# Attention rows, keys and skip weights as f16 high and low parts, with their splits and the early block sums on GpSimd

## The chip, the cores and the metric

The kernel runs on one core of a Trainium2 chip (trn2). The metric is the device time of one launch in microseconds (us), as the median of several executions. Engines are named as in the profile: PE is TensorE (matmuls), PEld its weight loads, DVE VectorE, ACT ScalarE, POOL GpSimd, SP SyncE, whose queue issues most DMAs.

## The reference

The input `x` is 16 batches of 128 channels by 1024 columns (f32), with a context of 128 by 256 for each. The first half is a cross-attention, the second a gated feed-forward with 4-bit weights:

```python
# x: (16, 128, 1024), ctx: (16, 128, 256), all weights of the attention 128 x 128
xn = layernorm(x)                                    # over the 1024 columns
q, k, v = Wq @ xn, Wk @ ctx, Wv @ ctx
att = softmax(q.T @ k / sqrt(128))                   # 1024 x 256 for each batch
x = x + Wskip @ xn + v @ att.T
h = silu(layernorm(x) @ Wg.T) * (layernorm(x) @ Wu.T)   # 2752 wide, dequantized weights
x = x + h @ Wd.T
```

## The kernel before, in words

The kernel has two phases. The attention phase goes through the 16 batches in steps 0 to 16 (`STEPS`), pipelined over the engines with an order written out by hand for each engine; semaphores join them. The feed-forward phase, some 1150 us of the span, multiplies in f16 high and low parts with a seven-product scheme for 2 by 2 blocks; the change does not touch it.

In step i of the attention phase, in program order on each engine:

- PE: `energies(i, 0)` (four products of 128 rows of the normalized batch, as weights, against 256 columns of keys), `block_transposed` of a "between" block, `values(i-1, 0)` (one skip product of 512 columns, L548, then two products with the transposed probabilities, L553), `energies(i, 1)`, `probs_transposed(i-1, 1)`, `keys_values(i+1)`, `block_transposed` of an "after" block, `values(i-1, 1)`, `probs_transposed(i, 0)`. The keys are folded with the query weights, so that energies need only the row `xn` and the keys `kk`.
- DVE: `maxima(i, 0)` (L1294), the sums and low parts of the "between" block (L1319, L1300), `normalize(1, i-2)` (L1277), `inverse_total(i, 0)` (L1336), `add_attention(i-1, 0)` (L1332), `normalize(0, i+1)` (L1277), `maxima(i, 1)`, `row_stats(0, i+2)` (L1263, L1267), in some steps a piece of the first feed-forward weights (`meanwhile`: two operations or one of 1024 elements in the steps 4 to 8 and 11 to 14), `inverse_total(i, 1)`, the sums and low parts of the "after" block, `add_attention(i-1, 1)`, `row_stats(1, i-1)`.
- ACT: `block_hi` of the between block, a cast of one block sum (`sum_hi`, L852), `exponentials(i, 0)` (L833), `normalize_probs(i, 0)` (L859), `probs_out(i-1, 1)` (L825), `exponentials(i, 1)`, `block_hi`, `keys_out(i+1)` (L815), another `sum_hi`, `values_out(i+1)` (L819), `probs_out(i, 0)`, `normalize_probs(i, 1)`. After steps 9 and 13 it casts feed-forward weights as well (L902, L904, L909).
- POOL: from step 5 on the low part of a block sum (`sum_lo`, L407), `inverse_deviation(0, i+2)` (L398, L401: the reciprocal deviation of the row two batches ahead, which waits for `row_stats(0, i+2)`), a second `sum_lo`, `inverse_deviation(1, i-1)`.
- SP: loads of rows and context, stores of finished rows.

Layout: `xn` has three buffers of 1024 f32 columns, the keys two of 256. `T1` to `T4` are the block sums of the feed-forward phase; each pair of batches k makes four of them, written by DVE as f32 into the last columns of their own f16 buffer (`mixed`), then cast (high part) and subtracted (low part).

## Time and profile before

| what | value |
|---|---|
| three runs | 1405.16, 1405.92, 1406.82 us, median 1405.92 us |
| span of the profiled execution, first to last instruction | 1403.7 us, 2.2 us below that median |
| PE busy | 1384.9 us (99%), 6414 matmul records |
| DVE busy | 1116.8 us (80%) |
| ACT busy | 689.1 us (49%) |
| POOL busy | 309.5 us (22%) |
| granted TensorE clock | 1.000 of 2.4 GHz |
| attention phase (steps 0 to 16) | about the first 215 us |

The profile lists an f32 matmul as two records of equal length, an f16 matmul as one. Instructions overlap at their ends, so that the distance from one start to the next is what an operation costs in a full stream. The profiled execution has no time of its own beside its span; the three runs are other executions, and the 2.2 us between the span and their median is what lies around the span.

### The profile page before, as it was taken

Reading aid. Unit: us, or ns where it says so; the run is one execution under the profiler, and the core shown is the slowest. Engines: PE = TensorE matmul, PEld = TensorE weight load, DVE = VectorE, ACT = ScalarE, POOL = GpSimd, SP = SyncE. Lnnn points to the kernel's source line nnn. Section 1 sums busy time; section 2 is a strip of 40 time slices with the busy share of each in tenths; the row PEclk is TensorE's granted clock in tenths of the full one; section 3 lists DMA queues with packets and bytes.
Section 4 is the critical chain, followed back from the end, with each engine's and each line's share of the span. In section 5 each row is a group of like instructions: output and inputs, shape, how many; then the busy total and the mean of one; then the engine's idle time right before and its main releaser. Section 6 shows DMA issues by size and latency. Waiting matters only on the chain.

```text
span 1403.7 us, 19579 instructions
## 1 busy us (share of the span) xinstructions
PE 1384.9 (99%) x6414; PEld 677.0 (48%) x6414; DVE 1116.8 (80%) x1598; ACT 689.1 (49%) x1279; POOL 309.5 (22%) x365
## 2 busy tenths in 40 slices
PE   8999998999999999999999999999999999999999
PEld 6676764444444444444444444444444444444443
DVE  6888978887877778878788788788788788787476
ACT  6899984344344444444444444444444444434430
POOL 1132332132122122122222212222212212212200
PEclk9999999999999999999999999999999999999999
DMA  5222222286477576576666756846846746848796
GB/s 191 102 102 87 83 91 61 53 158 120 98 143 126 103 137 115 101 143 112 119 130 113 131 111 115 148 94 123 133 105 122 125 104 121 141 91 150 121 303 256
DMA packets 58983, 174.83 MB, mean 125 GB/s; under 512 B 8001, under 2 KB 11073, under 8 KB 54593
## 3 DMA queue, kind: packets, MB, share of 16 engines
q0 software_dynamic: 34560, 83.90, 39.1%
q1 hardware_dynamic: 24096, 90.20, 20.7%
q8 instruction: 19, 0.31, 0.1%
q10 hardware_dynamic: 288, 0.26, 0.1%
q14 instruction: 20, 0.16, 0.0%
HBM read 73.67 MB, written 100.66 MB: 124 GB/s over the span
## 4 chain that ended last, share of the span: by engine, by line
PE 91%; DVE 4%; ACT 3%; issue 2%; POOL 0%; DMA 0%; SPq 0%; DVEq 0%; POOLq 0%; ACTq 0%
PE ps L590 52%; PE ps L629 9%; PE ps L628 9%; PE ps L630 9%; PE ps L553 3%; PE ps L523 2%; PE ps L793 2%; PE ps L511 2%; PE ps L548 1%; PE ps L542 1%; ACT temps L859 1%; ACT temps L833 1%; PE ps L752 1%; DVE stats L1263 0%; DVE neg_max L1294 0%
## 5 line engine op out<-in xcount | busy, mean ns | idle before, releaser
L590 PE MATMUL ps<-xt,w_gu 128*128 128x512 f16 x3528 | 796.1, 379 | 5.7 <-DVE temps L1510 1.7
L590 PEld LDWEIGHTS ps<-xt,w_gu 128*128 128x128 f16 x3528 | 344.6, 98 | 422.8 <-ACT temps L939 2.6
L972 ACT ACTIVATE stage<-ps,pow 128x512 f32<-128x512 f32 x300 | 204.2, 686 | 320.0 <-PE ps L630 318.3
L1540 DVE SCALAR_TENSOR_TENSOR stage<-ps,pow,stage 128x512 f32<-128x512 f32 x220 | 160.0, 746 | 101.3 <-ACT stage L972 63.0
L628 PE MATMUL ps<-park 128*128 128x512 f16 x560 | 212.3, 379 | 0.0
L629 PE MATMUL ps<-park 128*128 128x512 f16 x560 | 212.3, 379 | 0.0
L630 PE MATMUL ps<-park 128*128 128x512 f16 x560 | 212.3, 379 | 0.0
L437 POOL DMA_DIRECT2D out<-stage x80 | 70.5, 881 | 424.1 <-DVE stage L1540 424.1
L451 POOL DMA_DIRECT2D out<-stage x80 | 69.0, 863 | 297.4 <-ACT stage L972 297.4
L969 ACT CAST park<-temps 128x512 f16<-128x512 f32 x140 | 83.1, 614 | 64.8 <-DVE temps L1524 38.1
L1537 DVE TENSOR_TENSOR park<-temps,park 128x512 bf16<-128x512 f32 x140 | 98.3, 708 | 17.0 <-ACT park L969 14.0
L630 PEld LDWEIGHTS ps<-park 128*128 128x128 bf16 x560 | 54.8, 98 | 66.1
L628 PEld LDWEIGHTS ps<-park 128*128 128x128 f16 x560 | 54.7, 98 | 66.1
L629 PEld LDWEIGHTS ps<-park 128*128 128x128 f16 x560 | 54.7, 98 | 66.1
L444 POOL DMA_DIRECT2D out<-stage x60 | 66.2, 1103 | 4.8 <-DVE stage L1540 4.5
L523 PE MATMUL ps<-w_gu,park 128*128 128x256 f32 x256 | 60.5, 380 | 2.2 <-ACT w_gu L815 1.5
L833 ACT ACTIVATE temps<-ps,neg_max 128x256 f32<-128x256 f32 x128 | 58.9, 475 | 6.3 <-DVE neg_max L1287 3.8
L553 PE MATMUL ps<-temps,w_gu 128*128 128x512 f32 x128 | 60.3, 594 | 1.0 <-ACT temps L825 1.0
L467 POOL TENSOR_TENSOR temps<-temps 128x512 f32<-128x512 f32 x20 | 30.7, 1535 | 124.2 <-DVE temps L1530 124.2
L1396 DVE TENSOR_TENSOR w_gu<-raw,w_gu 128x1024 f16<-128x1024 f32 (+1 forms) x43 | 52.0, 1209 | 7.7 <-ACT w_gu L909 6.1
L859 ACT ACTIVATE temps<-temps,inv_total 128x256 f32<-128x256 f32 x128 | 54.7, 502 | 4.9 <-DVE inv_total L1336 4.9
L523 PEld LDWEIGHTS ps<-w_gu,park 128*128 128x128 f32 x256 | 47.4, 190 | 14.7 <-issue 7.2
(137 smaller groups left out, 1622.2 us busy)
## 6 DMA issues: line engine op xcount, KB each, us to landing
out<-stage POOLq DMA_DIRECT2D x80, 512.0 KB, 5.3
out<-stage POOLq DMA_DIRECT2D x140, 256.0 KB, 5.4
grid<-grids SPq DMA_DIRECT2D x136, 256.0 KB, 6.0
raw<-packed SPq DMA_DIRECT2D x34, 512.0 KB, 4.3
out<-stage SPq DMA_DIRECT2D x16, 512.0 KB, 2.7
stage<-x SPq DMA_DIRECT2D x12, 512.0 KB, 3.5
xt<-out SPq DMA_DIRECT2D x12, 512.0 KB, 11.7
out<-xt SPq DMA_DIRECT2D x12, 512.0 KB, 2.6
```

Of the source, the lines that this page charges most:

```text
L437: pool.dma_start(out[t, :, 0:NOUT], stage[:, d % 2, 0:NOUT], accum_op=ALU.add).then_inc(s_add11[d % 2], 16)
L523: mm = pe.matmul(ps_e[f][:, t, :], xn[b % XNS][:, cols], kk[:, par, :], start=True, stop=True)
L553: mm = pe.matmul(ps_o, v_t[:, par, h, :], prob_t[:, f, h, :], start=False, stop=(h == 1))
L590: mm = pe.matmul(bank, w_gu[e][:, wp, w, P * j:P * j + P], xt[:, xb, xp, j, cols], start=(fresh and n == 0), stop=(n == 3 * J - 1), skip_g ...
L628: pe.matmul(bank, h_hi[:, h, rows], w_d[:, 0, w, :], start=fresh, stop=False, skip_group_check=not fresh)
L629: pe.matmul(bank, h_hi[:, h, rows], w_d[:, 1, w, :], start=False, stop=False, skip_group_check=not fresh)
L630: return pe.matmul(bank, h_lo[:, h, rows], w_d[:, 0, w, :], start=False, stop=True, skip_group_check=not fresh)
L833: ex = act.activation(prob[:, NTH * f + t, :], ps_e[f][:, t, :], ACT.Exp, bias=neg_max[:, f, t:t + 1], accum_out=total[:, f, t:t + 1])
L969: act.copy(h_hi[:, block, :], src).then_inc(s_h_hi, 1)
L972: return act.activation(dst, ps[:, bank, :], ACT.Copy, scale=pow2[:, 10:11])
L1537: dve.tensor_tensor(h_lo[:, block, :], src, h_hi[:, block, :], ALU.subtract).then_inc(s_h_lo, 1)
L1540: return dve.scalar_tensor_tensor(out=part, in0=ps[:, bank, :], scalar=pow2[:, 10:11], in1=part, op0=ALU.mult, op1=ALU.add)
```

## The change

From batch 2 on (`SPLIT`) the attention keeps its operands as f16 pairs, a high part and what is left:

- The row: DVE's `normalize(0, b)` writes the f16 high part in place of the f32 row. POOL computes the f32 row again into a scratch area (`xn_exact`) and subtracts the high part from it (`split_row`).
- The keys: ACT writes f32 keys to a scratch area, POOL casts them (`kk_hi`) and subtracts (`kk_lo`), in `split_keys`.
- The skip weights are split once on POOL (`split_skip`).
- PE multiplies energies and skip as three f16 products each (high by high, low by high, high by low) in place of one f32 product. `energies(i+1, 0)` begins with a wait for `s_kk_hi`, then waits for `s_xn_lo` and `s_kk_lo` ahead of its second and third group.
- The high-part casts of the block sums of the first six pairs of batches go from ACT (`sum_hi`) to POOL (`sum_parts`). The other eight stay on ACT.
- Two waits for buffers: DVE's `bn_aggr` of row b waits until POOL has computed `xn_exact` of row b-2, and ACT's `keys_out(b)` until `kk_lo` of batch b-1 is done.

The core of the diff:

```diff
+            def split_row(b):
+                n = b - SPLIT + 1
+                hi, lo = xn_parts[b % XNS][:, 0, :], xn_parts[b % XNS][:, 1, :]
+                pool.wait_ge(s_rstd[0], b + 1)
+                wait(pool, s_xn_lo, n - 1)
+                pool.tensor_scalar(xn_exact, row(b).rearrange("p (c r) -> p c r", c=8), mv[:, 0, b % 2, 0:1],
+                                   rstd[:, 0, b % 2:b % 2 + 1], ALU.subtract, ALU.mult).then_inc(s_xn_exact, 1)
+                pool.wait_ge(s_xn, b + 1)
+                pool.wait_ge(s_xn_exact, n)
+                pool.tensor_tensor(lo.rearrange("p (c r) -> p c r", c=8), xn_exact,
+                                   hi.rearrange("p (c r) -> p c r", c=8), ALU.subtract).then_inc(s_xn_lo, 1)
+
+            def split_keys(b):
+                n = b - SPLIT + 1
+                hi, lo = kk_parts[:, b % 2, 0, :], kk_parts[:, b % 2, 1, :]
+                pool.wait_ge(s_kk_sb, b + 1)
+                pool.tensor_copy(hi, kk_exact).then_inc(s_kk_hi, 1)
+                pool.wait_ge(s_kk_hi, n)
+                pool.tensor_tensor(lo, kk_exact, hi, ALU.subtract).then_inc(s_kk_lo, 1)
...
+            def sum_parts(k, u):
+                pool.wait_ge(s_mixed, nth_sum(k, u) + 1)
+                pool.tensor_copy(xt_of(k, u, 0).rearrange("p j (h r) -> p j h r", h=2),
+                                 mixed(k, u).rearrange("p (j h) r -> p j h r", h=2)).then_inc(s_sum_cast, 1)
+                sum_lo(k, u)
...
             for i in range(1, STEPS):
                 k = (i - 5) // 2
                 if k >= 0:
-                    sum_lo(k, T2 if i % 2 == 0 else T3)
+                    sum_parts(k, T2 if i % 2 == 0 else T3)
+                if i + 1 < B:
+                    split_row(i + 1)
                 if i + 2 < B:
                     inverse_deviation(0, i + 2)
                 if i % 2 and k >= 0:
-                    sum_lo(k, T1)
+                    sum_parts(k, T1)
                 elif k >= 0:
-                    sum_lo(k, T4)
+                    sum_parts(k, T4)
+                if i + 1 < B:
+                    split_keys(i + 1)
                 inverse_deviation(1, i - 1)
...
+                n = b - SPLIT + 1
                 if f == 0:
-                    pe.wait_ge(s_kk_sb, b + 1)
                     pe.wait_ge(s_xn, b + 1)
+                    pe.wait_ge(s_kk_hi, n)
+                pe.wait_ge(s_exp, 2 * b + f - 1)
+                for xp, kp in ((0, 0), (1, 0), (0, 1)):
+                    if f == 0 and xp:
+                        pe.wait_ge(s_xn_lo, n)
+                    if f == 0 and kp:
+                        pe.wait_ge(s_kk_lo, n)
+                    for t in range(NTH):
+                        cols = slice(P * (NTH * f + t), P * (NTH * f + t) + P)
+                        mm = pe.matmul(ps_e[f][:, t, :], xn_parts[b % XNS][:, xp, cols], kk_parts[:, par, kp, :],
+                                       start=(xp + kp == 0 and t % 2 == 0), stop=(kp == 1), skip_group_check=True)
...
-                k = (i - 3) // 2
...
-                if k >= 1:
-                    sum_hi(k - 1, T1 if i % 2 else T4)
...
-                if i % 2 == 0 and k >= 0:
-                    sum_hi(k, T3)
-                elif k >= 1:
-                    sum_hi(k - 1, T2)
+                if i == B:
+                    sum_hi(LAST - 1, T3)
...
+                if which == 0:
+                    wait(dve, s_xn_exact, b - SPLIT - 1)
```

## Rows read from the trace of the kernel before

**Rows 1.** Busy time of each engine in the nine periods from step 5 to step 14
```profile
core 0: us, PE busy (x) PEld busy (x) DVE busy (x) ACT busy (x) POOL busy (x), PEclk, DMA share, GB/s
64.45:177.26 112.81, 111.75 (x524) 78.61 (x523) 100.81 (x206) 107.88 (x309) 39.51 (x54) 1.00 0.25 89
```

**Rows 2.** Pieces of the chain that ended last (start us, us, what)
```profile
130.85 0.52 ACT xt L852
...
179.65 1.88 ACT w_gu L909 x2
```

**Rows 3.** Timeline of PE: first energies of steps 2, 5, 9, 10, 11, 14, 15
```profile
28.10 1.89 PE L523 MATMUL ps<-w_gu,park 128*128 128x256 f32 x8
...
64.45 1.89 PE L523 MATMUL ps<-w_gu,park 128*128 128x256 f32 x8
...
114.11 1.89 PE L523 MATMUL ps<-w_gu,park 128*128 128x256 f32 x8
...
126.53 1.89 PE L523 MATMUL ps<-w_gu,park 128*128 128x256 f32 x8
...
140.02 1.89 PE L523 MATMUL ps<-w_gu,park 128*128 128x256 f32 x8
...
177.26 1.89 PE L523 MATMUL ps<-w_gu,park 128*128 128x256 f32 x8
...
191.17 1.89 PE L523 MATMUL ps<-w_gu,park 128*128 128x256 f32 x8
```

**Rows 4.** Timeline of PE: an f32 skip product, and twelve f16 products
```profile
116.31 1.02 PE L548 MATMUL ps<-park,w_gu 128*128 128x512 f32 x2
...
202.47 2.75 PE L590 MATMUL ps<-xt,w_gu 128*128 128x512 f16 x12
```

**Rows 5.** Timeline of step 9: DVE, POOL and ACT
```profile
116.24 1.17 DVE L1294 TENSOR_REDUCE neg_max<-ps 128x4 f32<-128x1024 f32 x1
...
117.25 1.16 POOL L407 TENSOR_TENSOR xt<-xt 128x512 f16<-128x512 f32 x1
...
118.52 0.81 DVE L1277 TENSOR_SCALAR park<-stage,mv,rstd 128x1024 f32<-128x1024 f32 x1
...
119.47 0.18 DVE L1336 RECIPROCAL inv_total<-total 128x4 f32<-128x4 f32 x1
...
120.14 0.81 DVE L1277 TENSOR_SCALAR park<-stage,mv,rstd 128x1024 f32<-128x1024 f32 x1
...
120.86 1.22 DVE L1294 TENSOR_REDUCE neg_max<-ps 128x4 f32<-128x1024 f32 x1
...
123.68 0.19 POOL L398 TENSOR_TENSOR var_eps<-mv,eps 128x1 f32<-128x1 f32 x1 [5.26 <-DVE mv L1267]
...
124.46 1.16 POOL L407 TENSOR_TENSOR xt<-xt 128x512 f16<-128x512 f32 x1
...
124.52 0.42 ACT L815 ACTIVATE w_gu<-ps 128x256 f32<-128x256 f32 x1
```

**Rows 6.** Timeline: DVE and POOL operations that overlap
```profile
86.21 1.18 DVE L1386 TENSOR_TENSOR raw<-raw,grid 128x1024 f32<-128x1024 int32 x1
...
86.44 1.00 POOL L398 TENSOR_TENSOR var_eps<-mv,eps 128x1 f32<-128x1 f32 x1 [6.13 <-DVE mv L1267]
...
149.79 0.46 POOL L398 TENSOR_TENSOR var_eps<-mv,eps 128x1 f32<-128x1 f32 x1 [5.22 <-DVE mv L1267]
...
150.32 1.42 POOL L401 TENSOR_TENSOR rstd<-var_eps,neg_half 128x1 f32<-128x1 f32 x1
...
206.91 1.15 POOL L407 TENSOR_TENSOR xt<-xt 128x512 f16<-128x512 f32 x1 [0.47 <-ACT xt L852]
...
207.55 1.06 DVE L1277 TENSOR_SCALAR park<-w_gu,mv,rstd 128x1024 f32<-128x1024 f32 x1
```

**Rows 7.** Timeline of POOL at the start: operations with one input or none
```profile
0.76 0.20 POOL L386 MEMSET ident<- 128x128 f32 x1
...
1.50 0.30 POOL L389 TENSOR_SCALAR_AFFINE_SELECT ident<-ident 128x128 f32<-128x128 f32 x1 [0.50 <-POOL eps L387]
```

More of the change, by code:

```diff
@@ L76, in nth_sum @@
     return 4 * k + SUMS.index(u)
+EARLY_SUMS = 4 * (LAST - 1)
 def uses_of_step(i):
@@ L97 @@
 XNS = 3
+SPLIT = 2
 LATER = 2
@@ L143, in build @@
         xn = [park[:, N * k:N * k + N] for k in range(3)]
+        xn_parts = [t.bitcast(F16).rearrange("p (a n) -> p a n", a=2) for t in xn]
         xn2 = park[:, 3072:7168].rearrange("p (s n) -> p s n", s=XNS2)
         x12 = more[:, :].rearrange("p (c r) -> p c r", c=8)
-        last_columns = xt[:, :, :, :, :].rearrange("p u a j t -> p u (a j) t").bitcast(F32)[:, :, :, (GT - P) // 2:]
+        xt_words = xt[:, :, :, :, :].rearrange("p u a j t -> p u (a j) t").bitcast(F32)
+        last_columns = xt_words[:, :, :, (GT - P) // 2:]
+        xn_exact = xt_words[:, X11, :, (GT - 2 * P) // 2:]
         def mixed(k, u):
@@ L223, in build @@
         s_xn = sem("s_xn")
+        s_xn_exact = sem("s_xn_exact")
+        s_xn_lo = sem("s_xn_lo")
+        s_kk_hi = sem("s_kk_hi")
+        s_kk_lo = sem("s_kk_lo")
+        s_skip_hi = sem("s_skip_hi")
+        s_skip_lo = sem("s_skip_lo")
+        s_sum_cast = sem("s_sum_cast")
         s_xn2 = sem("s_xn2")
@@ L410, in sum_lo @@
                                    ).then_inc(s_sum_lo, 1)
+            def sum_parts(k, u):
[3 more added lines that the diff above has]
+                sum_lo(k, u)
             inverse_deviation(0, 0)
             inverse_deviation(0, 1)
+            split_skip()
             inverse_deviation(0, 2)
@@ L516, in energies @@
                 par = b % 2
+                if b < SPLIT:
+                    if f == 0:
+                        pe.wait_ge(s_kk_sb, b + 1)
+                        pe.wait_ge(s_xn, b + 1)
+                    wait(pe, s_exp, 2 * b + f - 1)
+                    for t in range(NTH):
+                        cols = slice(P * (NTH * f + t), P * (NTH * f + t) + P)
+                        mm = pe.matmul(ps_e[f][:, t, :], xn[b % XNS][:, cols], kk[:, par, :], start=True, stop=True)
+                        if b == 0 and f == 0 and t == 1:
+                            mm.then_inc(s_first_energy, 1)
+                    mm.then_inc(s_energy, 1)
+                    return
+                n = b - SPLIT + 1
                 if f == 0:
-                    pe.wait_ge(s_kk_sb, b + 1)
                     pe.wait_ge(s_xn, b + 1)
-                wait(pe, s_exp, 2 * b + f - 1)
-                for t in range(NTH):
-                    cols = slice(P * (NTH * f + t), P * (NTH * f + t) + P)
-                    mm = pe.matmul(ps_e[f][:, t, :], xn[b % XNS][:, cols], kk[:, par, :], start=True, stop=True)
-                    if b == 0 and f == 0 and t == 1:
-                        mm.then_inc(s_first_energy, 1)
+                    pe.wait_ge(s_kk_hi, n)
[5 more added lines that the diff above has]
+                        pe.wait_ge(s_kk_lo, n)
+                    for t in range(NTH):
+                        cols = slice(P * (NTH * f + t), P * (NTH * f + t) + P)
+                        mm = pe.matmul(ps_e[f][:, t, :], xn_parts[b % XNS][:, xp, cols], kk_parts[:, par, kp, :],
+                                       start=(xp + kp == 0 and t % 2 == 0), stop=(kp == 1), skip_group_check=True)
                 mm.then_inc(s_energy, 1)
@@ L547, in values @@
                 wait(pe, s_res, 2 * b + f)
-                pe.matmul(ps_o, w_att[:, 3, :], xn[b % XNS][:, H * f:H * f + H], start=True, stop=False)
+                cols = slice(H * f, H * f + H)
+                if b < SPLIT:
+                    pe.matmul(ps_o, w_att[:, 3, :], xn[b % XNS][:, cols], start=True, stop=False)
+                else:
+                    if b == SPLIT and f == 0:
+                        pe.wait_ge(s_skip_lo, 1)
+                    for n, (wp, xp) in enumerate(((0, 0), (1, 0), (0, 1))):
+                        pe.matmul(ps_o, w_skip[:, wp, :], xn_parts[b % XNS][:, xp, cols], start=(n == 0), stop=False)
                 if f == 0:
@@ L814, in keys_out @@
                 act.wait_ge(s_kv, b + 1)
-                act.mul(kk[:, b % 2, :], ring_bank(("keys", b))[:, 0:M], float(C) ** -0.5).then_inc(s_kk_sb, 1)
+                wait(act, s_kk_lo, b - SPLIT)
+                act.mul(kk[:, b % 2, :] if b < SPLIT else kk_exact, ring_bank(("keys", b))[:, 0:M], float(C) ** -0.5
+                        ).then_inc(s_kk_sb, 1)
             def values_out(b):
@@ L1275, in normalize @@
                     dve.wait_ge(s_xt_ps, NTH_UNIT[(b - XNS2) // 2, X22 if b % 2 else X21] + 1)
-                dst, done = ((xn[b % XNS], s_xn), (xn2[:, b % XNS2, :], s_xn2))[which]
+                first = xn[b % XNS] if b < SPLIT else xn_parts[b % XNS][:, 0, :]
+                dst, done = ((first, s_xn), (xn2[:, b % XNS2, :], s_xn2))[which]
                 dve.tensor_scalar(dst, row(b), mv[:, which, b % 2, 0:1], rstd[:, which, b % 2:b % 2 + 1],
```

14 lines of the change are left out of this document (13 added, 1 removed).

## The prediction

> **What bounds the kernel now.** I read the page first, which says that PE is busy 99% of the span, then the stretches, then the chain of waits, then the timeline of one step. The change touches only the attention, so what counts is the limit there. In the nine periods from `energies(5, 0)` to `energies(14, 0)` PE is busy 111.75 of 112.81 us, ACT 107.88, DVE 100.81, POOL 39.51 [rows 1]: PE is the limit, but ACT is only 4% below it and DVE 11%. A regular period is 126.53 - 114.11 = 12.42 us [rows 3]. Two periods are longer, 10 (140.02 - 126.53 = 13.49) and 14 (191.17 - 177.26 = 13.91) [rows 3]: there the chain of waits leaves PE and runs through ACT, which also casts feed-forward weights, 1.88 us of them in the second case [rows 2]. The clock is granted in full throughout [rows 1]. So relief for PE is worth something only down to where the next loop through ACT, DVE and POOL closes. I therefore cost PE's gain, and then that loop.
>
> **What PE saves.** The records of an f16 product of 512 columns follow each other every (2.75 - 0.38) / 11 = 0.215 us (0.38 being one record), while an f32 product of 512 columns is two records in 1.02 us, 0.43 each after the overlap [rows 4]. So f32 costs four times f16, and three f16 products cost three quarters. Skip: 0.86 to 0.65, saving 0.21, twice a batch. Energies: eight f32 records of half the columns, 0.215 each, are 1.73 us (1.89 with the end of the last [rows 3]); twelve f16 products of 256 columns at half of 0.215 are 1.30, saving 0.43, twice a batch. The trace has no f16 product of 256 columns; the bounds are this half and, were weight loads to hold it, a third more (1.7, no saving at all on the energies). I take the half, from the nearest row, in which each product loads weights of its own too. Sum: 1.29 us a batch, 14 batches, 18 us, if PE stays the limit (period 11.13).
>
> **What ACT saves.** Two casts of 0.52 us a step [rows 2], so from 107.88 / 9 = 11.99 to 10.95 us a period [rows 1]. ACT is then no limit, and the extra casts after steps 9 and 13 fit into its slack: the 13.49 and 13.91 lose their excess.
>
> **What POOL gets.** Today 39.51 / 9 = 4.4 us a period [rows 1]. A subtraction of 512 elements takes 1.16 [rows 5] and one element 0.19 [rows 5], so 1.9 ns an element: 2.13 for `xn_lo` (1024), 0.67 for `kk_lo` (256). Operations with one input are shown only at 128 elements, 0.30 and 0.20 us [rows 7]; with 0.19 at one element that is 0.9 ns an element: 0.62 for a cast of 512, 0.40 for `kk_hi`, 1.06 for `xn_exact`. These prices are the least certain. From above they are bounded by the two-input price (1.16, 0.67, 2.13), from below by a third of mine. I take mine, as nearest to the one-input rows, but 1.3 for `xn_exact`, which has two operations in it and two scalars from memory. Sum with turnarounds: 4.4 + 1.24 + 1.3 + 2.13 + 0.40 + 0.67 + 0.3 = 10.4 us a period, under 12.4.
>
> The Trainium skill, GPSIMD Engine Reference, section 3.1, gives the two-input operation about 2.6 cycles an element at 1.2 GHz, which the 1.16 us for 512 agrees with, and a good one-input loop 1.8 cycles. By 1.8 cycles the cast would be 0.77 and `xn_exact` 1.54, and the period below would be 0.4 us longer, some 3 us in all.
>
> **The loop that POOL closes.** Occupancy is not the point; order is. `energies(i+1, 0)` now waits for `kk_hi`, which stands in POOL's queue behind `inverse_deviation(0, i+2)` and a whole `sum_parts`. That deviation waits for `row_stats(0, i+2)`, which stands on DVE behind `maxima(i, 1)`, and so back to `energies(i, 0)`. Every link is in program order, so the length of the loop is a floor of the period from step 5 on:
> - energies start to first maxima: 11 x 0.108 + 0.28 + 0.04 = 1.50.
> - First to second maxima, with exponentials, reciprocal, addition and normalization between: 120.86 - 116.24 = 4.62 [rows 5].
> - Second maxima to the deviation: 123.68 - 120.86 = 2.82 [rows 5].
> - The deviation: 124.46 - 123.68 = 0.78 [rows 5].
> - The cast of the sum and its turnaround: 0.70. Its low part: 1.10. `kk_hi` and its semaphore: 0.45.
>
> Together 11.97 us. Before, only the wait for ACT's keys (ready 8.7 us after the first maxima [rows 5]) stood there, and PE came later than that.
>
> **Locks.** DVE's normalization and a running POOL operation exclude each other: at 207.55 it lasts 1.06 in place of 0.81 and ends 0.55 after POOL's operation ends (208.06) [rows 6]. It goes the other way too: L398 takes 1.00 in place of 0.19 under a DVE operation with two SBUF inputs, and at 149.79 the two deviation instructions take together 1.14 longer [rows 6]. I walk the loop with that. POOL is free 1.0 us after the first maxima (117.25 against 116.24) and then casts and subtracts until 2.9. The first normalization, due at 2.3 (118.52), waits and ends at 3.45, which delays the reciprocal (3.2 before) by about 0.3. `xn_exact` runs from 3.45 to 4.75. The second normalization, due at 4.2, ends at 5.3, and the second maxima start at 5.35 in place of 4.62. That is 0.73 us: period 12.70. With `xn_exact` at 1.06 it is 0.48. The Trainium skill, SBUF — State Buffer, section "Who interferes with whom", calls this pair of ports an exclusive lock for a whole instruction and names both kinds of DVE operation; the rows agree.
>
> In steps 5 to 8 and 11 to 13 DVE's weight work follows `row_stats` directly and delays the deviation by 0.81 to 1.14 [rows 6]. Before that cost nothing, POOL having 8 us idle in a period; now it stands in the loop. Seven steps at 0.85 are 5.9 us. `xn_lo` ends about 7.5 after the first maxima, ahead of the deviation, and DVE's new wait for `xn_exact` of two rows back is met a step early: both nothing; if POOL ran a step late they would add to the same delay.
>
> **The sum.** Steps 5 to 14: 9 x 12.70 + 5.9 = 120.2 against 112.81: +7.4. Period 14 has no deviation of a row 16, so `kk_hi` waits only for ACT's keys: 1.5 + 0.73 + 8.7 + 0.5 = 11.4, taken 11.8 against 13.91: -2.1 (from -2.5 to -0.6 if ACT's extra casts are not hidden). Steps 2 to 4 have no sums on POOL, loop 10.2, but DVE, busy 100.81 of 112.81 anyway [rows 1], holds them: 36.35 us for three periods [rows 3], -1.0 (from 0 to -3.9). After `energies(15, 0)` PE saves up to 1.3, of which DVE, on which the first feed-forward blocks wait, lets half come through: -0.5. Elsewhere nothing: the feed-forward is unchanged and only shifts. `split_skip` is 0.7 us on idle POOL in step 0. Together +3.8 on the span of 1403.7. The median of the runs lies 2.2 above the span, so 1405.92 + 3.8 = 1409.7 us.
>
> **The rivals.**
> 1. PE stays the limit (the other side). The loop would have to be shorter than 11.13. For it: DVE and ACT busy times of 11.2 and 10.95 would nearly allow it. Against it: the links without any new operation are already 1.50 + 4.62 + 2.82 + 0.78 = 9.72, and `sum_lo` makes it 10.8; cast and `kk_hi` would have to take 0.3 together, and no lock may bite. Time: 1405.9 - 18 = 1388.
> 2. The loop is there, but short: one-input operations at a third of my price, `xn_exact` out of DVE's way, period 11.6. 9 x 11.6 + 5.9 = 110.3, -2.5; with the other terms -6.1: 1400.
> 3. POOL's one-input operations cost as much as its two-input ones: cast +0.54, `kk_hi` +0.27, `xn_exact` until 6.1 and so 2.05 of locks. Period 14.83; POOL's own sum is then 12.6 plus locks, so that it is nearly full as well. 9 x 14.83 + 5.9 = 139.4, +26.6, with the rest +23: 1429.
> 4. Gain and loss cancel, DVE setting the pace with its busy 11.2 plus locks of about 1: period 12.3 to 12.4, 1405.
>
> **Chances.** Forecast 46% (its own range 1404 to 1415), rival 1 10%, rival 2 17%, rival 3 22%, rival 4 5%. A change within 0.2% (2.8 us) can't be told from none. Faster: rival 1 and six tenths of rival 2, 20%. Same: rival 4, the rest of rival 2 and 10% of the forecast, 22%. Slower: 58%. The range leaves out rival 1 and half of rival 3: 1399 to 1429.
>
> **What the profile of the changed kernel would show.** PE's energies of batch 2 on as 12 records in about 1.5 us: right on the first term. Idle time of PE ahead of the energies' first product, released by POOL `kk_hi`, about 1.5 us in each step from 5 on: the loop. None there and starts 11.1 apart: rival 1. Casts of 512 at 0.6 and `xn_exact` at 1.3: the prices; at 1.2 and 2.1: rival 3. DVE's L1277 longer than 0.81 in most steps: the lock. L398 near 1.0 in steps 5 to 8 with a later start of the energies: the last term. The forecast is wrong above all if a one-input operation of POOL costs something else, for each 0.1 us of the cast is about 1 us of the time.

## The result, and the profile after

The changed kernel takes 1431.67 us (median of four runs, 1429.37 to 1431.8), the kernel before 1405.75 in its runs beside it. The ratio is 1.0179, 95% interval 1.0167 to 1.019: 26 us slower. I had forecast 1409.7 with a range of 1399 to 1429, so the sign was right and the size was not. The span of the profiled execution is 1427.6 us, 23.9 above that of before. That execution was the shortest of the four (1429.37 us, mean granted clock 0.994; the others took 1431.54 to 1431.8 at 0.990 or 0.991), so the traces below account for 23.9 of the 26 us; for the other two there is no trace. For the same reason differences of medians and differences of profiled spans are told apart below.

The busy line of the profile's page and the busy times of the nine periods (from `energies(5, 0)` to `energies(14, 0)`), columns as in [rows 1]:

```profile
PE 1376.8 (96%) x6554; PEld 670.8 (47%) x6554; DVE 1128.8 (79%) x1598; ACT 678.3 (48%) x1255; POOL 429.2 (30%) x447
```

```profile
74.51:201.81 127.30, 104.76 (x614) 73.09 (x612) 112.02 (x209) 103.09 (x297) 115.67 (x109) 0.99 0.24 83
```

Over the span PE is still the busiest by far. In the nine periods it isn't: PE 104.76, DVE 112.02, ACT 103.09 and POOL 115.67 of 127.30 us. No engine is at 100%, and POOL, 39.51 in [rows 1], has become the fullest.

The timeline of PE, first energies of steps 2, 5, 6, 9, 10, 11, 14 and 15 (some groups are cut by the window's end), against [rows 3]. The profile names no releaser for the waits in brackets ("issue"); which one it was is read from the program order and from what GpSimd does just then:

```profile
38.37 2.71 PE L600 MATMUL ps<-w_gu,park 128*128 128x256 f16 x12 [10.37 <-issue]
...
74.51 1.47 PE L600 MATMUL ps<-w_gu,park 128*128 128x256 f16 x12
...
90.50 2.72 PE L600 MATMUL ps<-w_gu,park 128*128 128x256 f16 x12 [3.31 <-issue]
...
93.63 0.81 PE L631 MATMUL ps<-park,w_gu 128*128 128x512 f16 x3
...
119.10 1.47 PE L600 MATMUL ps<-w_gu,park 128*128 128x256 f16 x12 [2.97 <-issue]
...
132.62 1.14 PE L600 MATMUL ps<-w_gu,park 128*128 128x256 f16 x9 [1.93 <-issue]
...
146.09 1.14 PE L600 MATMUL ps<-w_gu,park 128*128 128x256 f16 x9 [1.99 <-issue]
...
201.81 1.60 PE L600 MATMUL ps<-w_gu,park 128*128 128x256 f16 x10 [3.08 <-issue]
...
215.67 1.47 PE L600 MATMUL ps<-w_gu,park 128*128 128x256 f16 x12 [0.90 <-issue]
```

Where the 23.9 us are, by differences of these starts and those of [rows 3], beside my terms:

| stretch | before | after | difference | my term |
|---|---|---|---|---|
| up to energies 5 | 64.45 | 74.51 | +10.06 | -1.0 |
| nine periods | 112.81 | 127.30 | +14.49 | +7.4 |
| step 14 | 13.91 | 13.86 | -0.05 | -2.1 |
| from energies 15 to the end | 1212.53 | 1211.93 | -0.60 | -0.5 |

So three things have to be explained: ten microseconds ahead of step 5, where I had put one less, seven more than forecast in the steady steps, and two more than forecast in step 14. For the second, the timeline of POOL over step 9:

```profile
132.12 0.40 POOL L445 CAST w_gu<-w_gu 128x256 f16<-128x256 f32 x1
132.60 0.67 POOL L447 TENSOR_TENSOR w_gu<-w_gu 128x256 f16<-128x256 f32 x1
...
134.64 0.61 POOL L462 CAST xt<-xt 128x512 f16<-128x512 f32 x1
135.33 1.16 POOL L455 TENSOR_TENSOR xt<-xt 128x512 f16<-128x512 f32 x1
136.47 4.30 POOL L434 TENSOR_SCALAR xt<-stage,mv,rstd 128x1024 f32<-128x1024 f32 x1
140.92 2.13 POOL L438 TENSOR_TENSOR park<-xt,park 128x1024 f16<-128x1024 f32 x1
...
143.80 0.61 POOL L462 CAST xt<-xt 128x512 f16<-128x512 f32 x1
144.49 1.16 POOL L455 TENSOR_TENSOR xt<-xt 128x512 f16<-128x512 f32 x1
145.59 0.40 POOL L445 CAST w_gu<-w_gu 128x256 f16<-128x256 f32 x1
```

From `kk_hi` to `kk_hi` it is 145.59 - 132.12 = 13.47 us, the period of PE (146.09 - 132.62 = 13.47), with one gap of 0.59 in it; PE's energies start 0.50 after the start of `kk_hi` both times. From 78 us on POOL has no longer gap than 1.1 us up to the end of the nine periods: its queue is full. Casts (0.61, 0.40) and subtractions (0.67, 1.16, 2.13) cost what I had said. L434, the recomputed row `xn_exact`, costs 3.8 to 4.3 us where I had put 1.3.

For the first, the timeline of POOL at the start:

```profile
23.21 0.40 POOL L471 PARTITION_ALL_REDUCE pow_tmp<-pow  x1 [5.67 <-issue]
31.01 3.80 POOL L434 TENSOR_SCALAR xt<-stage,mv,rstd 128x1024 f32<-128x1024 f32 x1 [7.40 <-issue]
34.95 2.12 POOL L438 TENSOR_TENSOR park<-xt,park 128x1024 f16<-128x1024 f32 x1
...
37.88 0.40 POOL L445 CAST w_gu<-w_gu 128x256 f16<-128x256 f32 x1
```

The split of row 2 and of its keys stands in POOL's queue behind a reduction over the partitions (it finds the scales of the feed-forward weights), which has a gap of 5.67 us ahead of it and one of 7.40 behind it. `energies(2, 0)` starts 0.1 us after the end of `kk_hi`, at 38.37 in place of 28.10. GpSimd's sequencer (POOLq) has two instructions without busy time at the start of each gap: at 17.51 and 17.54, of the reduction's line, and at 23.56 and 23.60, of the line that comes next. The second pair, in the view of that line up to 36 us:

```profile
L434 POOLq MODIFY_POOL_CONFIG  x2: 83/83/83, 23.6 to 23.6; - x2
```

### The profile page after: what moved, and what is told of

Read it like the earlier page. It is cut to its first block, busy times and chain, and to the rows that moved or that the text cites. A ratio compares the mean times of both kernels' runs of the same rounds, so it can differ in the third digit from the quotient of the medians.

```text
span 1427.6 us, 19970 instructions
## 1 busy us (share of the span) xinstructions
PE 1376.8 (96%) x6554; PEld 670.8 (47%) x6554; DVE 1128.8 (79%) x1598; ACT 678.3 (48%) x1255; POOL 429.2 (30%) x447
## 4 chain that ended last, share of the span: by engine, by line
PE 88%; DVE 5%; issue 4%; ACT 2%; DMA 0%; POOL 0%; SPq 0%; DVEq 0%; POOLq 0%; ACTq 0%
PE ps L673 51%; PE ps L711 8%; PE ps L713 8%; PE ps L712 8%; PE ps L636 2%; PE ps L876 2%; PE ps L600 2%; PE ps L835 1%; PE ps L570 1%; PE ps L618 1%; PE ps L631 1%; DVE neg_max L1377 1%; ACT temps L918 1%; ACT temps L944 1%; DVE park L1360 1%
## 5 line engine op out<-in xcount | busy, mean ns | idle before, releaser
L600 PE MATMUL ps<-w_gu,park 128*128 128x256 f16 x336 | 44.3, 285 | 32.4 <-issue 32.4
L1377 DVE TENSOR_REDUCE neg_max<-ps 128x4 f32<-128x1024 f32 x31 | 37.5, 1211 | 25.2 <-PE ps L600 25.1
```

Source lines behind the costliest of these rows:

```text
L600: mm = pe.matmul(ps_e[f][:, t, :], xn_parts[b % XNS][:, xp, cols], kk_parts[:, par, kp, :], start=(xp + kp == 0 and t % 2 == 0), stop=(kp ...
```

## The experiments

All are edits of the changed kernel except where noted. The table gives the median, the ratio to the kernel before with its 95% interval, the start of `energies(5, 0)`, the length of the nine periods, and the busy times in them. The last column but one is PE's granted clock there.

| run | us | ratio | energies 5 | nine periods | PE | DVE | ACT | POOL | clock | what |
|---|---|---|---|---|---|---|---|---|---|---|
| after | 1431.67 | 1.0179 | 74.51 | 127.30 | 104.8 | 112.0 | 103.1 | 115.7 | 0.99 | |
| e1_split3 | 1423.71 | 1.0128 (1.0111 to 1.0144) | 64.95 | 131.35 | 109.8 | 111.8 | 103.3 | 115.5 | 0.93 | split from batch 3 |
| e11_no_reduce | 1420.36 | 1.0109 (1.0094 to 1.0124) | 63.31 | 128.97 | 107.5 | 111.5 | 103.0 | 115.1 | 0.96 | no reduction |
| e2_exact_dve | 1424.15 | 1.0138 (1.0121 to 1.0155) | 71.45 | 125.46 | 105.9 | 110.0 | 100.1 | 78.3 | 0.97 | row on DVE |
| e3_no_pool | 1400.23 | 0.9964 (0.995 to 0.9979) | 63.10 | 109.54 | 102.4 | 102.3 | 98.4 | 49.3 | 1.00 | no splits |
| e4_casts_act | 1423.96 | 1.0136 (1.0119 to 1.0153) | 74.99 | 119.97 | 103.8 | 108.8 | 107.4 | 102.9 | 1.00 | sums' casts on ACT |
| e5_keys_first | 1425.97 | 1.0143 (1.0126 to 1.016) | 75.08 | 124.48 | 103.9 | 118.4 | 101.8 | 115.0 | 1.00 | keys ahead of sum |
| e6_dve_three | 1410.94 | 1.0036 (1.0023 to 1.0048) | 64.56 | 116.94 | 103.4 | 111.1 | 97.7 | 76.7 | 1.00 | e1, e2, e5 together |
| e8_exact_act | 1414.33 | 1.0055 (1.0038 to 1.0071) | 67.88 | 118.14 | 104.5 | 101.4 | 108.6 | 79.9 | 0.99 | row on ACT, e1, e5 |
| e9_copy_exact | 1409.98 | 1.0033 (1.002 to 1.0046) | 63.87 | 118.33 | 103.6 | 105.7 | 100.7 | 88.1 | 1.00 | row as a copy, e1 |
| e10_casts_only | 1404.87 | 0.9994 (0.9985 to 1.0003) | 64.28 | 112.44 | 111.8 | 102.1 | 99.8 | 49.6 | 1.00 | before, casts on POOL |
| e12_row_cast | 1407.39 | 1.001 (1.0001 to 1.0019) | 65.89 | 116.01 | 103.6 | 109.6 | 99.4 | 86.8 | 1.00 | row cast, e1, e5 |

**The start (e1_split3).** Batch 2 stays f32:

```diff
-SPLIT = 2
+SPLIT = 3
...
-                if i + 1 < B:
+                if SPLIT <= i + 1 < B:
                     split_row(i + 1)
```

> The split begins with batch 3 in place of 2; nothing else. Theory A (two separate losses: at the start POOL's split of row 2 stands behind the all-reduce and the 7.4 us in which POOL does nothing after it; from step 5 on POOL's own queue of 13.5 to 14 us a step sets the period): energies(2, 0) start at about 28 us as before the change in place of 38.4, energies(5, 0) about 10 us earlier, the periods after step 5 unchanged near 14, time 1431.7 - 10 = 1421 us. Rival B (the wait only moves to row 3, since the same gap also delays POOL's deviations): energies(3, 0) still near 50 us, time 1429 us or more.

Energies 5 start 9.6 us earlier, as theory A had it, but only 8.0 us of time are gained (5.5 by the profiled spans), less than the 10 of theory A: the nine periods are 4.05 longer, with PE busy 5.0 us more for the same products. Its granted clock is 0.93. In steps 6, 8, 12 and 14 the twelve products that take 1.47 us at full clock take 2.72 after a wait; the row of step 6:

```profile
81.53 2.72 PE L600 MATMUL ps<-w_gu,park 128*128 128x256 f16 x12 [3.31 <-issue]
```

In the nine periods the changed kernel has one such step, step 6.

**The reduction (e11_no_reduce).** Batch 2 is split, but the reduction is a copy of the same six elements, which leaves out the maximum over the partitions:

```diff
-            pool.partition_all_reduce(pow2_tmp[:, 0:6], pow2[:, 0:6], P,
-                                      bass.bass_isa.ReduceOp.max).then_inc(s_extreme_all, 1)
+            pool.tensor_copy(pow2_tmp[:, 0:6], pow2[:, 0:6]).then_inc(s_extreme_all, 1)
```

> The changed kernel with the reduction over the partitions on GpSimd in the start replaced by a copy of the same 6 elements, so that the scales of the weights are those of each partition and the output is not the reference's. Everything else as changed, the split of row 2 too. Theory A (the stall of the start is the 7.40 us that GpSimd waits for nothing visible after that reduction, and belongs to the reduction): the recomputed row starts right behind DVE's normalization, near 24.3 us in place of 31.0, energies 2 near 31.5 in place of 38.4, and the time falls by 6 to 7 us, to 1425. Theory H (the gap is something else of the first split of a row, a load of the code of that operation for example): a gap of several us stays ahead of the recomputed row, energies 2 at 36 or later, and less than 3 us are gained.

It gains 11.3 us (9.6 by the profiled spans: energies 5 start 11.2 earlier, and the nine periods, at a mean clock of 0.96, are 1.7 longer). That is the whole delay of the start and more than theory A gave. The timeline of POOL and that of PE:

```profile
19.01 3.79 POOL L434 TENSOR_SCALAR xt<-stage,mv,rstd 128x1024 f32<-128x1024 f32 x1
24.00 2.13 POOL L438 TENSOR_TENSOR park<-xt,park 128x1024 f16<-128x1024 f32 x1 [1.20 <-DVE park L1359]
```

```profile
27.97 1.47 PE L599 MATMUL ps<-w_gu,park 128*128 128x256 f16 x12 [0.24 <-issue]
```

With the reduction both gaps have gone, 5.67 us ahead of it and 7.40 behind, and with them both pairs of `MODIFY_POOL_CONFIG`. I had counted only the second gap. The row is recomputed at 19.01 in place of 31.01, ahead of DVE's own normalization, and PE has practically no wait. The stall of the start is shown to belong to the reduction and to the split being queued behind it.

**What POOL's operations cost (e7_pool_ops).** A kernel of its own, POOL the only engine that computes, three of each at 1024 f32 columns (two of each of the shorter ones), and no other part of the computation:

```python
pool.tensor_scalar(dst, row, a, b, ALU.subtract, ALU.mult)   # L63 as in the kernel, L65 plain layout
pool.tensor_scalar(dst, row, a, None, ALU.subtract)          # L67
pool.tensor_copy(dst, row)                                   # L73; L75 to f16
pool.tensor_tensor(dst, row, row, ALU.subtract)              # L77
pool.tensor_scalar(dst[:, 0:w], row[:, 0:w], a, b, ...)      # L80, w = 512, 256, 128
```

> A kernel of its own: POOL alone works on a row of 128 x 1024 f32 in a row of operations, each waited for, with DVE, ACT and PE idle; the rest of the computation is left out, the output is a copy of x, and its time as a whole says nothing. It gives the price of xn_exact in parts: both operations with scalars from memory into a strided area (as in the changed kernel), the same into a dense one, one operation only, scalars in the instruction, copies, cast, subtraction, shorter rows. Theory F (the 4.0 us are POOL's own work, by the scalars from memory or by the second operation): about 3.8 us here too, and one of the two makes most of it. Rival C (the 4.0 us are waiting for DVE): 1.1 to 1.5 us here. After an all-reduce the next ordinary operation starts some 7 us late.

Groups of instructions (line, engine, operation, shapes, count; busy us, mean ns of one; idle before), and two rows of its timeline:

```profile
L63 POOL TENSOR_SCALAR wide<-row,two 128x1024 f32<-128x1024 f32 x3 | 11.4, 3789 | 11.5 <-issue 11.3
L67 POOL TENSOR_SCALAR dst<-row,two 128x1024 f32<-128x1024 f32 x3 | 8.5, 2846 | 0.3
L77 POOL TENSOR_TENSOR dst<-row 128x1024 f32<-128x1024 f32 x3 | 5.7, 1893 | 0.2
L75 POOL CAST half<-row 128x1024 f16<-128x1024 f32 x3 | 3.1, 1043 | 0.2
L73 POOL COPY dst<-row 128x1024 f32<-128x1024 f32 x3 | 3.1, 1039 | 0.2
L80 POOL TENSOR_SCALAR dst<-row,two 128x128 f32<-128x128 f32 x2 | 1.6, 796 | 0.2
```

```profile
91.18 0.40 POOL L82 PARTITION_ALL_REDUCE dst<-row  x1 [5.93 <-issue]
91.64 1.04 POOL L83 CAST half<-row 128x1024 f16<-128x1024 f32 x1
```

The recomputation costs 3.79 us with no other engine computing beside it, so neither locks nor the scratch area's layout make it slow: it is the price of the operation. The number of inputs says nothing here. A copy with one input takes 1.04, a subtraction with two 1.89, one arithmetic operation with a scalar 2.85, two of them 3.79. From 128 to 1024 columns the last grows by (3.79 - 0.80) / 896 = 3.3 ns an element. Theory F was right on the size, but neither of its two parts makes most of it: the second operation costs 0.94 us, and the scalars from memory 0.15 against scalars in the instruction (3.63). The expected gap behind the reduction didn't come; the one ahead of the first did (5.93), and the second reduction had none. The trace has a pair of `MODIFY_POOL_CONFIG` ahead of the first reduction, at 85.44 and 85.48, and none behind either.

**The row as a copy (e9_copy_exact).** From batch 3 on, with the recomputation replaced by a plain copy, so that this scratch row is not normalized:

```diff
-                pool.tensor_scalar(xn_exact, row(b).rearrange("p (c r) -> p c r", c=8), mv[:, 0, b % 2, 0:1],
-                                   rstd[:, 0, b % 2:b % 2 + 1], ALU.subtract, ALU.mult).then_inc(s_xn_exact, 1)
+                pool.tensor_copy(xn_exact, row(b).rearrange("p (c r) -> p c r", c=8)).then_inc(s_xn_exact, 1)
```

> The changed kernel with f16 parts from batch 3 on, and the recomputation of the row on GpSimd replaced by a plain copy of the row (1.04 us for 1024 elements by the bench kernel), so the normalization is left out of that scratch row and the low part is not the real one; every other operation, wait and order stays. This gives the operation the price that my prediction assumed (1.3 us). Theory A (the forecast failed on this one price and on the start; its loop and locks are right): the nine periods from energies 5 to energies 14 come to 9 x 12.45 + 5.9 = 118 us (12.45 being 11.97 plus locks of 0.48), energies 5 at 65, time 1409 us, between 1406 and 1412. Theory C (GpSimd's queue is too long and too often locked whatever this operation costs): nine periods of 122 us or more, 1415 us or more. Theory F (locks and weight steps were over-counted): nine periods of 114 or less, 1404 or less.

It gives the operation a price near the one I had assumed (1.04 us; I had taken 1.3), and the time is 1409.98, nine periods 118.33: theory A. Window, POOL, DVE and PE in step 9:

```profile
63.87:182.20 118.33, 103.62 (x614) 72.36 (x612) 105.68 (x209) 100.68 (x294) 88.08 (x109) 1.00 0.25 88
```

```profile
118.94 1.23 DVE L1376 TENSOR_REDUCE neg_max<-ps 128x4 f32<-128x1024 f32 x1 [0.37 <-PE ps L599]
...
121.28 1.58 DVE L1359 TENSOR_SCALAR park<-stage,mv,rstd 128x1024 f32<-128x1024 f32 x1
...
124.17 1.21 DVE L1376 TENSOR_REDUCE neg_max<-ps 128x4 f32<-128x1024 f32 x1
```

```profile
121.28 1.04 POOL L434 COPY xt<-stage 128x1024 f32<-128x1024 f32 x1
...
126.98 0.19 POOL L416 TENSOR_TENSOR var_eps<-mv,eps 128x1 f32<-128x1 f32 x1 [0.52 <-DVE mv L1348]
...
127.75 0.61 POOL L461 CAST xt<-xt 128x512 f16<-128x512 f32 x1
128.44 1.16 POOL L454 TENSOR_TENSOR xt<-xt 128x512 f16<-128x512 f32 x1
129.54 0.40 POOL L444 CAST w_gu<-w_gu 128x256 f16<-128x256 f32 x1
```

```profile
130.04 1.14 PE L599 MATMUL ps<-w_gu,park 128*128 128x256 f16 x9 [0.54 <-issue]
```

From energies at 117.43 the links are 1.51 to the first maxima, 5.23 to the second, 2.81 to the deviation, 0.77 for it, 0.69 + 1.10 for the sum, 0.50 for `kk_hi`: 12.61. In this run, other than in that step of the changed kernel, POOL waits for the deviation (0.52), so the loop and not POOL's queue sets the period.

**The row on DVE (e2_exact_dve).** DVE computes it, right behind its normalization, and POOL's recomputation is left out:

```diff
+                if which == 0 and b >= SPLIT:
+                    wait(dve, s_xn_lo, b - SPLIT)
+                    dve.tensor_scalar(xn_exact, row(b).rearrange("p (c r) -> p c r", c=8), mv[:, 0, b % 2, 0:1],
+                                      rstd[:, 0, b % 2:b % 2 + 1], ALU.subtract, ALU.mult).then_inc(s_xn_exact, 1)
```

> The f32 row xn_exact is computed by DVE (one more tensor_scalar of 1024 a step) in place of POOL; POOL only subtracts. Theory A: POOL's queue loses 4.15 us a step and is no longer full, DVE gains 0.7 to 0.8; the period falls from 14.1 to between 12.4 and 13.0 and the start shortens by about 4 us: 1431.7 - 9 x 1.4 - 4 = 1415 to 1418 us. Rival C (the 4.0 us of xn_exact on POOL are mostly waiting for DVE's lock, and the lock is what costs): DVE's additional operation takes as much time away again, period stays above 13.7, time 1427 us or more.

POOL falls to 78.3 us, but the time only by 7.5, to 1424.15: between the two expectations. Step 9 is down to 141.41 - 128.68 = 12.73 us. Energies 5 still start at 71.45, since the low part of row 2 stays behind the reduction, and the energies of two steps of the nine, 6 and 12, are at half clock (2.72 us; 0.97 on average). The row isn't free on DVE either, where it is one more operation of 0.8 us a step.

**The order on POOL (e5_keys_first).** The keys are split ahead of the second block sum:

```diff
+                if i + 1 < B:
+                    split_keys(i + 1)
                 if i % 2 and k >= 0:
                     sum_parts(k, T1)
                 elif k >= 0:
                     sum_parts(k, T4)
-                if i + 1 < B:
-                    split_keys(i + 1)
```

> POOL splits the keys ahead of the second block sum of a step, in place of behind it; the amount of work is the same. Theory A (from step 5 on POOL's queue is full, its work of some 13.5 us a step sets the period): no change, 1429 to 1433 us, the mean of the nine periods from step 5 within 0.3 us of 14.1. Rival E (what counts is the way to the cast of the keys, as in the prediction's loop, and it gets 1.9 us shorter in each of 9 steps): 1414 to 1418 us.

Neither, by the time: 5.7 us less by the medians, 3.5 by the profiled spans, of them 2.8 in the nine periods and 0.8 in step 14. The mean period, 13.83 us, is just within the 0.3 of theory A. POOL does the same work (115.0) and is as full, which another order doesn't change. The energies of steps 6 and 14 are at full clock here; whether the gain is that or the keys' earlier place isn't shown.

**The casts (e4_casts_act, e10_casts_only).** e4 gives the casts of the block sums back to ACT (`EARLY_SUMS = 0`, `sum_lo` in place of `sum_parts`, `sum_hi` in ACT's steps as before). e10 is the kernel before with those casts alone moved to POOL:

```diff
+            def sum_parts(k, u):
+                pool.wait_ge(s_mixed, nth_sum(k, u) + 1)
+                pool.tensor_copy(xt_of(k, u, 0).rearrange("p j (h r) -> p j h r", h=2),
+                                 mixed(k, u).rearrange("p (j h) r -> p j h r", h=2)).then_inc(s_sum_cast, 1)
+                sum_lo(k, u)
```

> The casts of all block sums go back to ACT, the splits stay on POOL. Theory A: POOL's queue loses 2 x 0.69 us a step, and as it sets the period, the period falls from 14.1 to 12.7 over some 10 steps: 1431.7 - 12 = 1418 to 1421 us, the start unchanged (energies(2, 0) at 38.4). Rival C (locks between DVE and POOL cost, not the length of the queue): at most half of it, 1425 us or more.

> The kernel before, with the one part of the change that moves the casts of the block sums of the first six pairs from ScalarE to GpSimd; rows, keys and skip weights stay f32. Theory A (a cast of 0.6 us on GpSimd is free while GpSimd is busy 4.4 of 12.4 us, TensorE stays the limit, and ScalarE's excess in steps 10 and 14 goes): regular periods 12.42 as before, steps 10 and 14 shorter by up to 1.1 and 1.5 us, time 1403.2 us, between 1402.3 and 1404.5. Theory L (the casts lock DVE's normalization often enough, and the low parts now stand ahead of the deviation for longer): periods of 12.5 to 12.7 and 1406 us or more.

e4 gains 7.7 us by the medians, between theory A and rival C; by the profiled spans it is 6.0, made of 7.3 in the nine periods, 0.6 in step 14 and 2.0 lost ahead of step 5 and behind step 14. In the nine periods POOL, which is full, is rid of (115.67 - 102.94) / 9 = 1.4 us a period, and more than half of it reaches the period. In e10 the same casts cost nothing (POOL is busy 49.6 us) and gain 0.7 us, which can't be told from none: it falls between A and L. Step 10 is 13.05 us and step 14 is 13.48, 0.44 and 0.43 less than in [rows 3], not 1.1 and 1.5 less. The chain of waits shows what still holds them, ACT's casts of feed-forward weights, in period 10 and in period 14:

```profile
128.74 0.51 ACT w_gu L910
129.25 0.95 ACT w_gu L912
...
179.10 1.88 ACT w_gu L917 x2
```

**What the relief of PE is worth (e3_no_pool).** PE multiplies the high parts three times; low parts of rows, keys and skip weights aren't computed, and POOL keeps only the block sums:

```diff
-                    split_row(i + 1)
...
-                    split_keys(i + 1)
...
-                        mm = pe.matmul(ps_e[f][:, t, :], xn_parts[b % XNS][:, xp, cols], kk_parts[:, par, kp, :],
+                        mm = pe.matmul(ps_e[f][:, t, :], xn_parts[b % XNS][:, 0, cols], kk_parts[:, par, 0, :],
```

> POOL splits neither rows, keys nor skip weights: ACT writes the keys as f16 at once, and PE multiplies the high parts three times, so the low parts are left out of energies and skip. The products, their number and the casts of block sums on POOL stay. Theory A (PE's saving is real and only POOL's splits hide it): PE's period falls to between 11.1 and 11.6, 14 batches x 1.29 = 18 us less than before the change, less what DVE holds back: 1388 to 1394 us. Rival D (the three f16 products are themselves no gain, by weight loads or waits between them): 1404 us or more.

1400.23 us: 5.4 less than before, where A had 1388 to 1394 and D 1404 or more, so neither. PE is busy 102.4 us in the nine periods, 9.4 less than in [rows 1], but they last 109.54, only 3.3 less. Two neighbouring periods are 11.38 and 12.49 long, and the longer has this wait in the timeline of PE:

```profile
119.29 0.72 PE L607 MATMUL ps<-ident,park 128*128 128x128 f32 x4 [1.07 <-ACT temps L898]
```

PE waits for `probs_out` on ACT (6.9 us in the nine periods), and ACT for DVE's maxima (4.9) and reciprocals (3.2). That next loop, read from these waits, through ACT and DVE, is 11.9 us as a mean of such a pair, and 109.54 / 9 = 12.2 over all nine.

**Three ways to build it better (e6_dve_three, e8_exact_act, e12_row_cast).** All from batch 3 on and with the keys first. e6 computes the row on DVE as e2, e8 on ACT from a negative mean made on POOL. In e12 DVE writes the f32 row to the scratch area in place of the high part, and POOL casts it:

```diff
-                pool.tensor_scalar(xn_exact, row(b).rearrange("p (c r) -> p c r", c=8), mv[:, 0, b % 2, 0:1],
-                                   rstd[:, 0, b % 2:b % 2 + 1], ALU.subtract, ALU.mult).then_inc(s_xn_exact, 1)
-                pool.wait_ge(s_xn, b + 1)
                 pool.wait_ge(s_xn_exact, n)
+                pool.tensor_copy(hi.rearrange("p (c r) -> p c r", c=8), xn_exact).then_inc(s_xn, 1)
+                pool.wait_ge(s_xn, b + 1)
```

> Three edits together: split from batch 3 on, xn_exact on DVE, keys split ahead of the second sum. Theory A: the start is as before the change and POOL's loop is 10.9 us, 11.8 with weight work, below DVE's; the period is the one of the run without POOL's splits (109.5 / 9 = 12.2 with everything) plus DVE's additional 0.7, near 12.7: nine periods 113 to 116 us, time 1405 to 1409 us, no better than before the change. Rival E (POOL's splits cost by themselves, wherever they stand): 1415 us or more.

> Split from batch 3 on, keys split ahead of the second sum, and xn_exact on ACT, as an activation with scale and bias, for which POOL makes the negative product of mean and reciprocal deviation (two operations of one element). ACT has the time that its casts left free. Theory A: DVE's period of 12.2 (with weight work) stays, ACT's work is 10.95 + 0.95 = 11.9 us a step and just fits; nine periods 110 to 113 us, time 1400 to 1405 us. Rival G (ACT is then as full as before and each of its waits counts): nine periods 114 us or more, 1407 us or more.

> The whole computation, with the split made without recomputing the row: DVE's normalization writes the f32 row into the scratch area in the 0.8 us that it takes in either form, GpSimd casts it to the high part (1.04 us for 1024 elements by the bench kernel) and subtracts for the low part (2.13). f16 parts from batch 3 on, and the keys split ahead of the second block sum. Theory A (what slowed the changed kernel is the 4 us recomputation on GpSimd and what stood behind it; without both, DVE and ScalarE set the pace as in the run without splits, 11.94 us a period, plus locks of 0.3 to 0.5): nine periods of 110 to 113 us, time 1400.5 to 1405, so the kernel before or slightly less. Theory L (locks between GpSimd's casts and subtractions and DVE's operations cost what TensorE's relief brings, and energies now also wait for GpSimd's cast of the row): nine periods of 115 us or more, 1406 us or more.

They give 1410.94 (2 above A's range), 1414.33 and 1407.39. e8 missed A, and rival G had it: ACT, relieved of the casts, is filled again (108.6). e12 recovers 24 of the 26 us, yet ends 1.2 us above the kernel before, inside theory L's range. The locks of L are there: in eight of its nine periods one of DVE's normalizations, begun beside a subtraction of POOL, takes 1.11 to 1.73 us in place of 0.81. Waits in its nine periods (engine, line, what it waited for: us in total, times, longest):

```profile
PE ps L615 <- ACT temps L907: 10.1, 9, 1.6
...
ACT temps L915 <- DVE neg_max L1379: 7.8, 8, 1.7
```

PE waits 1.1 us in each step for ACT's transposed probabilities, and ACT for DVE's maxima: the loop of e3, its mean over the nine periods lengthened from 12.2 to 116.01 / 9 = 12.9 us. DVE is busy 109.6 us against 102.3 in e3. No version that does the whole computation beat the kernel before by more than can be measured.

## Why the prediction was wrong

- **The step that failed: the price of `xn_exact`.** I took 1.3 us and bounded it with "From above they are bounded by the two-input price (1.16, 0.67, 2.13)". The bound was no bound: the operation costs 3.79 (e7), 3.8 to 4.3 in place. The nearest rows were a memset and a select of 128 elements [rows 7], and neither does arithmetic with scalars from memory on f32 data. The Trainium skill, GPSIMD Engine Reference, section 3.1, gives 1.8 cycles an element at 1.2 GHz as the best case of a tight loop, by estimate 1.54 us here. The measurement decides: the 3.79 us are 4.4 such cycles an element.
- **What followed from it.** I summed POOL to 10.4 us a period, "under 12.4". With 3.8 to 4.3 in it the same sum is 12.9 to 13.4, over 12.4; measured are 13.47 and 12.54 in the two periods without weight work, 9 and 10. Rival 3 had the consequence ("nearly full as well") at a price of 2.1 and gave 1429, nearest to what came, but by luck: its condition was false (casts and `kk_hi` cost 0.61 and 0.40), and it came there by locks more than by occupancy. With a copy at 1.04 us in its place the terms of the nine periods hold: e9 has 118.33 us against 9 x 12.45 + 5.9 = 118.0. From e9 to the changed kernel it is 127.30 - 118.33 = 8.97 us; my miss, 127.30 - 120.2 = 7.1, and the 2.2 that I had given for 1.3 in place of 1.06 us make 9.3. So this one price accounts for the error in the nine periods, with the stretch at half clock in step 6 that e9 doesn't have. Against e1, which like e9 begins with batch 3 and has three such stretches inside the nine periods, it is 131.35 - 118.33 = 13.0. That e9 as a whole (1409.98) meets the forecast (1409.7) is luck in part: step 14 gives 1.2 less than my term, and the nine periods take 1.9 less than my 7.4.
- **The step that was missing: the start.** I wrote "steps 2 to 4 have no sums on POOL, loop 10.2", and looked at the loop but not at what stood ahead of it in POOL's queue. The gap behind the reduction (7.38 us) was in the trace of the kernel before, where only the deviations of later rows waited in it. In the changed kernel `energies(2, 0)` waits for what stands behind. Cost: 10.3 us at step 2, 10.06 by step 5, where my sum had -1.0; e11 gives all of it back with the recomputation as slow as before. At 11.1 us it is the larger of the two misses and independent of the first.
- **PE's saving** was right in its terms: energies 1.47 us, skip 0.81 for three records. PE's busy time in the nine periods falls by less than the 9 x 1.29 = 11.6 of my sum: by 7.0 in the changed kernel, part of it at half clock, and by 9.4 in e3. What it is worth is another matter: with nothing added elsewhere it brings 5.4 us (e3), not the 18 of rival 1, since the loop through ACT and DVE closes at 11.9 us. I had said that the relief counts "only down to where the next loop closes", and e3 measures it.
- **The loop and the weight steps** were right where POOL isn't full. e9: 12.61 and 12.83 us in steps 9 and 10, against 12.45, and on average 13.27 in the seven weight steps, against 12.45 + 0.85 = 13.30.
- **The locks** were right under subtraction and copy, only in part under the recomputation. In e9 the first normalization takes 1.58 us, begun with a copy of POOL and ended 0.54 after it. Beside L434 of the changed kernel, in the nine periods, DVE's normalizations take 0.80 to 1.11 us and L434 0.2 to 0.5 us more than its 3.79 in eight of nine cases: DVE mostly goes on and POOL pays (below).
- **Period 14, -2.1:** measured -0.05. In e5, the same work at full clock, it is 13.02, and in e9 13.01, so 0.9 of the term was there. In the changed kernel its mean clock is 0.88, after a wait of 3.08 us, and the ten products of the energies shown above take 1.60 us; that is the likely cause of the other 0.85, which no run tried by itself. For the 1.2 that are missing even at full clock, e10 shows that the sums' casts were only 0.43 of the old excess; ACT's extra casts still stood in its chain.

```profile
201.81:215.67 13.86, 12.94 (x68) 8.92 (x69) 11.20 (x14) 10.67 (x31) 12.91 (x11) 0.88 0.39 88
```

- **The tail, -0.5:** measured -0.6.
- **The clock** I took for granted in full. In the changed kernel the stretch of the energies of step 6 is at 0.50, its lower level of 1.2 GHz, after a wait of 3.31 us:

```profile
90.50:93.02 2.52, 2.52 (x13) 1.79 (x13) 0.00 (x0) 0.00 (x0) 2.36 (x5) 0.50 0.00 0
```

  Such a stretch makes up to 2.72 us of 1.47; the energies of step 2 (2.71 us after a wait of 10.37) and a part of step 14 have it too. In the nine periods that is little in the changed kernel (0.99) and more in e1 (0.93; PE busy 5.0 more, periods 4.05 longer). That the clock alone makes those 4.05 us was not tried by itself.
- **Left open:** what the 7.4 us behind the reduction are spent on. It isn't the recomputation as the next operation: in the kernel before, an operation on one element comes next, and the gap is 7.38. In all twelve kernels with the gap (7.0 to 8.5 us) the pair of `MODIFY_POOL_CONFIG` stands at its start; the small kernel, with a cast next, has no pair behind its reductions and no gap, and e11 has neither. So the gap goes with that pair; no run put a cast behind the reduction in the whole kernel to try it.

## What to carry to other kernels

An operation that the trace of the kernel before doesn't contain has no price from rows of other operations on the same engine: on GpSimd a copy and a recomputation lay a factor of 3.6 apart at the same size and the same number of inputs. Before work is put on an idle engine, its queue has to be read as well as its load, from the first instruction on, for once a critical product waits for that queue, each gap in it counts. And the relief of a bounding engine is worth no more than the distance to the next loop, here 3.3 of the 9.4 us in nine periods.

## What the runs showed of the hardware

- GpSimd, 128 x 1024 f32: copy 1.04 us, cast to f16 1.04, subtraction of two tensors 1.89, tensor-scalar with one operation 2.85 and with two 3.79. Immediates in place of scalars from memory change little (2.78 and 3.63), nor does the layout (3.78).
- The first reduction over partitions has a gap of 5.5 to 5.9 us ahead of it in every kernel here that has one, with two `MODIFY_POOL_CONFIG` at the start of the gap, and the second has neither. The Trainium skill, GPSIMD Engine Reference, section 2.1, states about 6 us for the first call of a freshly loaded routine; the 5.93 us agree.
- Two normalizations of DVE inside one recomputation on GpSimd, changed kernel, step 9: neither is longer than 0.81 us, and GpSimd's operation, begun at 136.47, takes 4.30 us in place of 3.79.

```profile
136.47 0.80 DVE L1360 TENSOR_SCALAR park<-stage,mv,rstd 128x1024 f32<-128x1024 f32 x1
...
138.03 0.81 DVE L1360 TENSOR_SCALAR park<-stage,mv,rstd 128x1024 f16<-128x1024 f32 x1
```

  The Trainium skill, SBUF — State Buffer, section "Who interferes with whom", has whoever issues first hold the shared ports for the whole instruction, while the other waits. Copy and subtraction behave so (1.58 us above, and 1.06 in [rows 6]). This operation doesn't in step 9: the second normalization runs in its midst. In step 3 of the same trace it goes the other way, L434, begun at 54.13, takes its 3.79 us and both normalizations are long; what decides isn't shown.

```profile
54.18 1.69 DVE L1360 TENSOR_SCALAR park<-stage,mv,rstd 128x1024 f32<-128x1024 f32 x1
...
56.94 1.52 DVE L1360 TENSOR_SCALAR park<-w_gu,mv,rstd 128x1024 f16<-128x1024 f32 x1
```

- TensorE's granted clock fell to its lower level, 1.2 GHz, after some waits and not after others of the same length: after 3.31 us in the changed kernel and in e1, not in e11; after 3.65 us in e1 (energies 12, 2.72 us), not in the changed kernel (1.47); after 1.77 us in e2 once (energies 6) and once not (energies 7). The length of the wait alone doesn't tell.
